# Experts over dispatched token blocks in plain fp32, rows scattered and added back by indirect DMAs

## The reference

```python
logits = x @ gate_weight.T                      # 1024 tokens, 28 experts
scores = softmax(logits)
topk_w, topk_idx = top_k(scores, 6)
topk_w = topk_w / (topk_w.sum(-1) + 1e-20)
cw = zeros(1024, 28); cw[token, topk_idx] = topk_w
for e in 28 experts:                            # w_gate, w_up 256x176, w_down 176x256
    h = silu(x @ w_gate[e]) * (x @ w_up[e])
    y = y + cw[:, e] * (h @ w_down[e])
```

## Time and profile before

| | us |
|---|---|
| median of 3 runs | 1101.35 |
| lowest, highest | 1100.94, 1104.36 |
| profiled execution | 1102.48 |
| its span | 1100.7 |
| PE busy in the span | 923.4 (84%) |
| DVE, ACT, POOL busy | 583.1, 399.9, 501.0 |
| 16 DMA engines, mean moved | 70 GB/s |

### The profile page before, as it was taken

The page is one execution under the profiler, slowest core; times in us unless marked ns, Lnnn a source line. Parts: engine busy times, 40 slices in busy tenths (PEclk is TensorE's granted clock), DMA queues, the critical chain, the costliest instruction groups (busy, mean ns, idle before and its releaser), DMA issues. The chain is left out here.

```text
span 1100.7 us, 14919 instructions
## 1 busy us (share of the span) xinstructions
PE 923.4 (84%) x5205; PEld 692.6 (63%) x5206; DVE 583.1 (53%) x1343; ACT 399.9 (36%) x1042; POOL 501.0 (46%) x492
## 2 busy tenths in 40 slices
PE   5898989885588876786898758998998988999998
PEld 3566766653457544554565436766766777888887
DVE  2367697965473885354475233554446464334333
ACT  2255554541022110231232113444444534444443
POOL 2256666752030233113124123455344556788875
PEclk9799989987689887779798758999999989999999
DMA  8030000022200200000000103333223324454442
GB/s 292 0 154 2 1 1 1 1 77 115 77 0 1 99 5 15 1 6 14 1 10 10 21 1 106 96 121 96 73 96 96 98 80 151 144 161 151 159 155 93
DMA packets 47103, 76.52 MB, mean 70 GB/s; under 512 B 21252, under 2 KB 24629, under 8 KB 46134
## 3 DMA queue, kind: packets, MB, share of 16 engines
q1 hardware_dynamic: 46308, 75.20, 21.4%
q10 hardware_dynamic: 722, 0.37, 0.1%
HBM read 73.35 MB, written 2.21 MB: 69 GB/s over the span
## 5 line engine op out<-in xcount | busy, mean ns | idle before, releaser
L791 PE MATMUL PS<-R 128*64 128x256 f32 (+7 forms) x992 | 141.1, 378 | 13.9 <-ACT R L1990 8.4
L1990 ACT ACTIVATE R<-PS 128x512 f32<-128x512 f32 (+5 forms) x183 | 87.8, 519 | 131.1 <-PE PS L791 72.6
L2418 POOL TENSOR_TENSOR R<-SelT,bqkv 128x1024 f32<-128x1024 f32 x32 | 64.2, 2027 | 155.3 <-DVE SelT L1810 93.2
L791 PE MATMUL PS<-xTh,uh 128*128 128x512 f32 x312 | 130.9, 420 | 2.1 <-POOL ul L2430 2.0
L791 PE MATMUL PS<-xTh,ul 128*128 128x512 f32 x312 | 124.8, 400 | 0.0
L791 PE MATMUL PS<-xTl,uh 128*128 128x512 f32 x312 | 124.7, 400 | 0.0
L2430 POOL TENSOR_TENSOR ul<-R,uh 128x512 fp32r<-128x512 f32 x78 | 100.6, 1290 | 37.8 <-ACT uh L1990 37.7
L791 PEld LDWEIGHTS PS<-R 128*64 128x64 f32 (+3 forms) x992 | 75.1, 158 | 65.5 <-issue 32.2
L799 PE MATMUL PS<-ident,R 128*128 128x128 f32 (+2 forms) x462 | 74.7, 299 | 49.5 <-ACT R L2232 22.4
L2351 POOL TENSOR_SCALAR R<-R 128x256 f32<-128x256 f32 x88 | 80.9, 937 | 61.8 <-DVE R L1508 61.8
L799 PEld LDWEIGHTS PS<-ident,R 128*128 128x128 f32 (+2 forms) x462 | 55.2, 151 | 73.9 <-ACT R L2232 31.3
(11 more groups left out here) (280 smaller groups left out, 1968.6 us busy)
## 6 DMA issues: line engine op xcount, KB each, us to landing
R<-in_wmo SPq DMA_DIRECT2D x78, 384.0 KB, 3.1
xh<-cwd SPq DMA_DIRECT2D x28, 256.0 KB, 3.3
R<-in_wqkv SPq DMA_DIRECT2D x1, 4096.0 KB, 13.2
xh<-cwd SPq DMA_DIRECT2D x14, 224.0 KB, 3.1
xh<-cwd SPq DMA_DIRECT2D x14, 192.0 KB, 3.1
xh<-cwd SPq DMA_DIRECT2D x14, 160.0 KB, 3.0
R<-in_wot SPq DMA_DIRECT2D x1, 2048.0 KB
bqkv<-in_bqkv SPq DMA_DIRECT2D x1, 2048.0 KB, 7.9
```

Source lines behind the costliest of these rows:

```text
L791: return e.matmul(out, l, r, start=start, stop=stop, skip_group_check=True)
L1990: return e.activation(out, a, ACT.Copy)
L2418: e.tensor_tensor(pv4(pr2, i % 2, "ghd"), Pg, vg, ALU.mult).then_inc(sem("m2"), 1)
```

## The change

The experts are computed only for the tokens that chose them. The chosen (token, expert) pairs are 1024 x 6 = 6144 rows. Each batch's router now finds the six indices (`max_index`), counts ranks with small matmuls (`rk`), works out each row's place in DRAM (`rt_p`) and scatters the rows of 258 words (256 features, the weight, the token's number) by 12 indirect DMAs on POOL (`sc`) into `xg`, where each expert has room for 1024 rows. SP fills `xg` and three accumulators `y0` to `y2` with blank rows at the start of the program (32 DMAs). `mp` works out, from the counts, which expert and which rows belong to each of 75 blocks of 128 rows; 75 = 48 full blocks + 27 is the most that there can be, and all 75 are run. A block's result is added to `y{j%3}` in DRAM by one indirect DMA with an add. At the end SP loads the three, DVE adds them to x.

`moe`, `l1x_late` and the split operands are gone. The cross attention of all four batches stands in one `l1x` beside `l1a` (ratio 0.8), and the experts follow it alone.

```diff
-NCH = 39
+NB = 75
+NW = 3
+NX = 8
+NY = 3
+    def experts():
+        add("mp", banks=[0, 1, 7])
+        for j in range(NX - 2):
+            add("ldx", j)
+        for j in range(NW):
+            add("ldw", j)
+        add("et", 0, banks=[0])
+        add("et", 1, banks=[1])
+        add("eu", 0, banks=[2])
+        for j in range(NB + 1):
+            if j + NX - 2 < NB:
+                add("ldx", j + NX - 2)
+            if j + 1 < NB:
+                add("eu", j + 1, banks=[2 + (j + 1) % 2])
+            if j < NB:
+                add("eh", j, banks=[4 + j % 2])
+            if j:
+                add("ed", j - 1, banks=[6 + (j - 1) % 2])
+                if j - 1 + NW < NB:
+                    add("ldw", j - 1 + NW)
+            if j + 2 < NB:
+                add("et", j + 2, banks=[j % 2])
+        add("out")
...
-    side = drive(l1x((0, 1), extra_), side, 0.75)
+    side = drive(l1x((0, 1, 2, 3), extra_), side, 0.8)
-    side = drive(moe(0), second(), RATIO)
-    drive(moe(1), None, 0)
+    experts()
...
 # SP
+            for ex in range(NE):
+                dst = D["xg"][ex * CAP:ex * CAP + CAP, :].rearrange("(c p) n -> p c n", p=128)
+                e.dma_start(dst, zrow[:, :].rearrange("p (o n) -> p o n", o=1).to_broadcast([128, 8, ROW])).then_inc(sem("init"), 16)
+            def ldx(j):
+                if j == 0:
+                    e.wait_ge(sem("blocks"), 1)
+                    e.wait_ge(sem("xg"), 16 * 48)
+                if j >= NX:
+                    i = j - NX
+                    e.wait_ge(sem(f"y{i % NY}"), 16 * (i // NY + 1))
+                r = e.value_load(blocks[0:1, 128 + j:129 + j], min_val=0, max_val=PAD)
+                e.dma_start(xb[j % NX], D["xg"][bass.ds(r, 128), :]).then_inc(sem(f"xb{j % NX}"), 16)
+            def ldw(j):
+                if j >= NW:
+                    u = fill("ed", j - NW)
+                    e.wait_ge(u.full, u.f + 1)
+                v = e.value_load(blocks[0:1, j:j + 1], min_val=0, max_val=NE - 1)
+                e.dma_start(wr_[j % NW], D["wgu"][bass.ds(v, 1)].rearrange("o p n -> (o p) n")).then_inc(sem(f"w{j % NW}"), 16)
+                e.dma_start(wr2[j % NW], D["wd2"][bass.ds(v, 1)].rearrange("o p n -> (o p) n")).then_inc(sem(f"w{j % NW}"), 16)
...
 # PE
+            def et(j):
+                u = fill("et", j)
+                e.wait_ge(sem(f"xb{j % NX}"), 16 * (j // NX + 1))
+                room(u)
+                for c in range(2):
+                    a = tr(u.t[:, c * 128:c * 128 + 128], xb[j % NX][:, c * 128:c * 128 + 128])
+                a.then_inc(u.full, 1)
+            def eu(j):
+                u, w = fill("eu", j), fill("et", j)
+                e.wait_ge(w.free, w.k + 1)
+                e.wait_ge(sem(f"w{j % NW}"), 32 * (j // NW + 1))
+                room(u)
+                for k in range(2):
+                    a = mm(u.t[:, 0:352], xbT[j % 2][:, k, :], wr_[j % NW][:, 352 * k:352 * k + 352], k == 0, k == 1)
+                a.then_inc(u.full, 1)
+            def eh(j):
+                u, w = fill("eh", j), fill("eu", j)
+                e.wait_ge(w.free, w.k + 1)
+                room(u)
+                tr(u.t[:, 0:128], hm[j % 2][:, 0:128])
+                tr(u.t[0:48, 128:256], hm[j % 2][:, 128:176]).then_inc(u.full, 1)
+            def ed(j):
+                u, w = fill("ed", j), fill("eh", j)
+                e.wait_ge(w.free, w.k + 1)
+                room(u)
+                mm(u.t[:, 0:256], hT_[j % 2][:, 0:128], wr_[j % NW][:, 704:960], True, False)
+                mm(u.t[:, 0:256], hT_[j % 2][0:48, 128:256], wr2[j % NW], False, True).then_inc(u.full, 1)
...
 # DVE: eu multiplies silu(gate) by up, eh copies hT_, ed scales by the token's weight
+            def ed(j):
+                u = fill("ed", j)
+                e.wait_ge(u.full, u.f + 1)
+                if j >= NY:
+                    e.wait_ge(sem(f"y{j % NY}"), 16 * (j // NY))
+                e.tensor_scalar(ys[j % NY], u.t[:, 0:256], xb[j % NX][:, 256:257], None, ALU.mult).then_inc(u.free, 1)
...
 # ACT: et copies xbT, eu takes silu of the gate half
...
 # POOL
+            def ed(j):
+                u = fill("ed", j)
+                e.wait_ge(u.free, u.k + 1)
+                if j >= NY:
+                    e.wait_ge(sem(f"y{j % NY}"), 16 * (j // NY))
+                e.indirect_dma_start(out=D[f"y{j % NY}"][:, :],
+                                     out_offset=bass.IndirectOffsetOnAxis(ap=xb[j % NX][:, 257:258].bitcast(I32), axis=0),
+                                     in_=ys[j % NY], in_offset=None, compute_op=ALU.add).then_inc(sem(f"y{j % NY}"), 16)
```

More of the change, by code:

```diff
@@ L58, in pair_banks @@
 def pair_banks(i):
[L60 to L71, removed]
+    return ((2, 3), (4, 5))[i % 2]
 def plan():
@@ L307, in ask @@
             for b in bs:
-                if b not in asked and b in x3:
+                if b not in asked and b in x3 and b <= now + 1:
                     asked.append(b)
@@ L339, in l1x @@
                 yield
[L341 to L358, removed]
     def done(b, p, extra_):
@@ L408, in plan @@
     extra_ = []
-    side = drive(l1x((0, 1), extra_), side, 0.75)
-    for _ in side or ():
-        pass
-    while 1 not in cwc:
+    side = drive(l1x((0, 1, 2, 3), extra_), side, 0.8)
+    assert side is None
+    while extra_:
         if next(extra_[0], "end") == "end":
             extra_.pop(0)
[L415 to L421, removed]
-    side = drive(moe(0), second(), RATIO)
-    for _ in side or ():
-        pass
-    drive(moe(1), None, 0)
+    experts()
     return p
@@ new lines, in mp @@
+            def mp():
+                u0, u1, u7 = fills("mp")
+                e.wait_ge(sem("SM"), 4)
+                room(u0)
+                mm(u0.t[0:28, 0:1], SM, ones[:, 0:1], True, True).then_inc(u0.full, 1)
+                e.wait_ge(sem("blk_n"), 1)
+                room(u1)
+                mm(u1.t[0:28, 0:1], utri2[0:28, 0:28], mpn[:, 1:2], True, True).then_inc(u1.full, 1)
+                e.wait_ge(u1.free, u1.k + 1)
+                room(u7)
+                mm(u7.t[0:1, 0:75], ones[0:28, 0:1], mpb, True, True)
+                mm(u7.t[0:1, 128:203], mpn[:, 2:3], mpb, True, True).then_inc(u7.full, 1)
@@ L1892, in rt_k @@
                 u = fill("rt_g", b)
+                e.wait_ge(u.free, u.k + 1)
                 got = [None, None]
-                def step(s, ins):
-                    own.mark(ins)
+                for s in range(2):
+                    own.mark(e.max(m8b[:, s, :], p30[s]))
                     got[s] = own.n
-                def after(s):
+                for s in range(2):
                     e.wait_ge(own.sem, got[s])
-                for s in range(2):
-                    if s == 0:
-                        e.wait_ge(u.free, u.k + 1)
-                    step(s, e.reciprocal(rr[s][:, 2:3], rr[s][:, 1:2]))
@@ L1918, in rt_k @@
-                for s in range(2):
-                    after(s)
-                    step(s, e.tensor_reduce(rr[s][:, 3:4], r30[s][:, 0:28], X, ALU.add))
-                for s in range(2):
-                    after(s)
-                    step(s, e.tensor_scalar(rr[s][:, 3:4], rr[s][:, 3:4], 1e-20, None, ALU.add))
-                for s in range(2):
-                    after(s)
-                    step(s, e.reciprocal(rr[s][:, 3:4], rr[s][:, 3:4]))
-                for s in range(2):
-                    if s == 0 and b:
-                        w = fill("rt_c", b - 1)
-                        e.wait_ge(w.full, w.f + 1)
-                    after(s)
-                    e.tensor_scalar(cwr[s], r30[s][:, 0:28], rr[s][:, 3:4], None, ALU.mult).then_inc(sem("cwr"), 1)
@@ L1963, in out @@
-            def out(hf):
-                us = fills("y0", hf)
-                e.wait_ge(sem("dn"), NCH * (hf + 1))
-                for q in range(2):
-                    t0 = 4 * hf + 2 * q
-                    xv_ = x[:, t0:t0 + 2, :]
-                    e.tensor_tensor(xv_, us[q].t[:, :].rearrange("p (q n) -> p q n", q=2), xv_, ALU.add).then_inc(us[q].free, 1)
+                    own.mark(e.max_index(ix8[:, s, :], m8b[:, s, :], p30[s]))
+                own.mark(e.tensor_reduce(rq[:, 0:2], m8b[:, :, 2:8], X, ALU.add))
@@ new lines, in ed, with out @@
+            def ed(j):
+                u = fill("ed", j)
+                e.wait_ge(u.full, u.f + 1)
+                if j >= NY:
+                    e.wait_ge(sem(f"y{j % NY}"), 16 * (j // NY))
+                e.tensor_scalar(ys[j % NY], u.t[:, 0:256], xb[j % NX][:, 256:257], None, ALU.mult).then_inc(u.free, 1)
+            def out():
+                for i in range(NY):
+                    e.wait_ge(sem(f"yb{i}"), 16)
+                    for q in range(4):
+                        xv_ = x[:, 2 * q:2 * q + 2, :]
+                        a = e.tensor_tensor(xv_, yb[i][:, 2 * q:2 * q + 2, :], xv_, ALU.add)
+                        if i < NY - 1:
+                            own.mark(a)
+                        else:
```

(13 more changed lines are left out.)

439 lines of the change are left out of this document (198 added, 241 removed).

## The result

| | us |
|---|---|
| before, median (lowest to highest) | 1102.86 (1100.94 to 1106.71) |
| after, median (lowest to highest) | 1510.12 (1506.61 to 1517.83) |
| after / before, 95% interval | 1.370 (1.363 to 1.376) |
| profiled execution of after, its span | 1510.95, 1508.9 |

The changed kernel is 37% slower. The forecast of 1400 us was 110 us too low; the time lies within its range. Matmuls now have line L757, transposes L765.

The account below looks back on a forecast made before the run. The prediction took PE to bound the dense experts before, and exposed weight loads to pace blocks after: blocks start at 760, plus 622 for 75 blocks and 15.5 tail, 1397, plus 1.8, called 1400 us; range from a little under 1220 to 1535.

Parts of the forecast that it names:

- 75 blocks: The expert block stage: 75 periods of 8.3 us, 622 us in all.
- The ring: Weights' ring of three places: nothing is fetched ahead, so each block pays the full way from `ed`'s end to landing.
- The landing way: In each block, from `ed`'s end to landed weights: semaphore 0.1, register 0.8, loads 3.5, together 4.4 us.
- The block's work: PE's `eu`, `eh` and `ed` in each block: 2.3 us at 2.4 GHz, divided by clock 0.6, 3.8 us.
- Rival 1: Block stage: PE's clock stays at 1.2 GHz throughout, 9.1 us a block, 1461 us in all; chance 20%.
- The start of the blocks: Everything ahead of the expert blocks, from cross attention through routers, scatters and first loads: blocks start at 760 us.
- 16 x 5.6: Cross attention of batches 2 and 3: 16 pairs at 5.6 us, 90 us; longer pairs would mean being wrong.
- The 5 us for all side effects: Ahead of the last scatter: POOL's scatters of batches 0 to 2 before norms, and 33 MB of blank rows; 0 to 20.
- Scatter and first loads: Before the first block: batch 3's 12 scatters with landing 15 us, then SP's first x and weight loads 12 us.
- Rival 2: Block stage: adding DMAs bind through SP's queue, deciding from a y way of 7.2 us; 1580 at 12; chance 15%.
- rival 3: Block stage: landings at their shortest and full clock, 5.9 us a block, 1220 us in all; chance 10%.
- Rival 4: Block stage: the ring hides the loads and PE sets about 3.4 us a block, 1033 us; chance 4%.

Follow-up runs that it names:

- ring6: Changed kernel with six places instead of three in the ring of weights: 1095.94 us, 0.991 of the kernel before.
- fixed_expert: Changed kernel with block j always taking expert j mod 28, so no register read for the weights: 1454.77 us, 1.317 of the kernel before.
- warm16: Changed kernel with sixteen unused bf16 matmuls on PE in the gap ahead of each `eu`: 1359.28 us, 1.231 of the kernel before.
- ring6_spread: ring6 with the 12 scatters of a batch issued one by one between cross attention steps: 1072.95 us, 0.971 of the kernel before.
- no_add: Changed kernel with block results written to y by the indirect DMAs without the add: 1529.13 us, 1.385 of the kernel before.
- ring4: Changed kernel with four places instead of three in the ring of weights: 1228.83 us, 1.112 of the kernel before.
- all_together: ring6 with spread scatters, `et` ahead of `eh`, and first weights asked ahead of the first x rows: 1056.01 us, 0.955 of the kernel before.
- all_x_later: all_together with x rows asked for four blocks ahead, not six: 1031.35 us, 0.936 of the kernel before.

## Why the prediction was right, and where it was off

It was right in kind: slower, because each block exposes its whole load. Its sum (1400) was 111 us short of the profiled 1510.95, and the wide range covered that. By its own parts:

| part | forecast | measured | difference |
|---|---|---|---|
| first `eu` | 760 | 805.4 | +45.4 |
| 75 blocks | 622 | 685.5 | +63.5 |
| tail to the end of the span | 15.5 | 18.0 | +2.5 |

**The ring.** Right. `ldw(n)` waits for `ed(n-3)`, and between that and `eu(n)` stands one `et`. ring6 takes that away alone, and 414 us go.

**The landing way, 4.4 us and 0.1 for the start.** Right: 4.47 in the middle of the blocks. Its terms hold as well: the register 0.67 to 0.71 (0.8 forecast, by fixed_expert), the two loads 3.5 (3.5).

**The block's work, 3.8 us.** This step failed: the work took 4.75 us in the mean, and these 0.95 us are nearly all of the period's excess. Both numbers of 2.3 / 0.6 were off. The sum of matmuls at the higher clock was short: warm16 shows 2.64 for the same burst. Most of that is `ed`, sized 0.85, which takes 1.16 there (1005.64 to 1006.80 in one block), since its last matmul has to be through. 2.64 / 0.6 = 4.4, an estimate by which this is 0.6 of the 0.95 us. The rest is the clock. The stage's mean was forecast well (0.6; 0.61 measured), but a mean over a stage holds the gaps as well, and a grant that falls into a gap gives nothing back. Windows of after: `eu` with `eh`, `ed`, the wait, and the next `eu`; then the same three of the second block after:

```profile
1207.10:1210.00 2.90, 2.90 (x7) 1.75 (x7) 0.00 (x0) 0.18 (x1) 0.00 (x0) 0.50 0.13 25
1210.00:1211.60 1.60, 1.60 (x7) 0.83 (x6) 0.83 (x4) 0.13 (x1) 0.00 (x0) 0.85 0.17 56
1212.40:1216.00 3.60, 0.00 (x0) 0.00 (x0) 0.00 (x0) 0.00 (x0) 1.41 (x1) 0.71 0.74 180
1216.10:1219.00 2.90, 2.90 (x7) 1.75 (x7) 0.00 (x0) 0.18 (x1) 0.00 (x0) 0.50 0.16 33
...
1225.40:1228.30 2.90, 2.90 (x7) 1.75 (x8) 0.00 (x0) 0.20 (x1) 0.00 (x0) 0.50 0.17 32
1228.30:1230.40 2.10, 2.10 (x5) 0.82 (x4) 0.73 (x3) 0.12 (x1) 0.00 (x0) 0.50 0.13 41
1230.50:1234.70 4.20, 0.61 (x2) 0.21 (x2) 0.48 (x1) 0.38 (x1) 1.55 (x1) 0.50 0.55 147
```

In the first of these blocks `eu` runs at 1.2 GHz (0.50), the higher clock is granted late in the burst (0.85), lasts into the wait (0.71), and is gone when the next `eu` starts. In the last block shown it isn't granted at all. So it goes throughout: of the 70 blocks from 829.95 us on, all have 0.50 or 0.51 over the first 2.9 us, and 30 have 0.50 to the end of the wait. The mean clock is 0.54 in the bursts and 0.68 in the gaps. By form the mean matmul of `eu` takes 826 / 478 = 1.73 times as long as in warm16, those of `ed` 609 / 428 = 1.42 and 578 / 380 = 1.52. So the work of a block came near the 4.6 that the prediction had for 1.2 GHz throughout (bursts that stay at 0.50 take 5.04). Rival 1 (9.1 us a block, given 20%) was nearer than the forecast (8.3). The Trainium skill's section "HAM oscillation — how this bites in real kernels" ("TensorE: Matmul & The Clock Gate") has PE restart throttled after each wait for DMA, and the trace agrees (0.50 or 0.51 in the first 2.9 us of each of these 70 bursts).

75 times the excess of the period, 9.29 - 8.3, would be 74 us. 63.5 came of it, since the first three loads are asked for together and only the later blocks wait for `ed`. The `eu` of blocks 0, 1 and 2 in after:

```profile
805.37 2.69 PE L757 MATMUL PS<-R,bqkv 128*128 128x352 f32 x4 [6.68 <-issue]
...
808.70 2.69 PE L757 MATMUL PS<-R,bqkv 128*128 128x352 f32 x4 [0.65 <-issue]
...
812.71 2.33 PE L757 MATMUL PS<-R,bqkv 128*128 128x352 f32 x4 [0.47 <-ACT bqkv L1997]
```

The first two periods take 7.3 us together, 11.2 less than two of 9.29. Nothing is saved at the end: from the last `eu` (1480.93) to the end of the last `ed` 10.0 us pass.

**The start of the blocks, 760.** The pairs were sized well: 5.7 and 5.2 us each within batches 2 and 3 (5.6 forecast). Wrong was 16 x 5.6: from the last pair of one batch to the first of the next, PE's `xs` steps are 39.3 us apart (590.39 to 629.69, batch 1 to 2) and 36.4 (669.91 to 706.36, batch 2 to 3), and the sum had 5.6 for each. So the 16 pairs took 152 us (590.39 to 742.49), 9.5 each, and more than 5.6 each was what the prediction had named as a sign of being wrong. Of the two distances, 16.4 and 18.1 us are the waits behind POOL's scatters; in ring6_spread the same distances are 26.8 and 20.4. The rest, 13 to 17 us each above a pair's 5.6, is `x_end`, norm and router of one batch and `x_pre` of the next, which the prediction costed for the last batch alone. Batch 1 being through 15 us sooner (its last pair starts at 590.39, not at 605.69 as in the earlier trace rows) gave some of it back. The 5 us for all side effects named the right queue and priced it at a seventh of its cost: it did not work out who waits behind twelve scatters in a row. The 33 MB of blank rows, in the same charge, cost nothing that shows: wqkv lands at 144 us, DMA is quiet from slice 5 on (151 us), and POOL's first product of the self attention starts at 392.7 us, 1.5 sooner than before.

**Scatter and first loads.** Right in sum: from the last `xs` to the first `eu` 64 us were forecast, 62.9 measured. A scatter's issue takes 0.96 us and 0.30 to the next, 1.27 in all (1.0 forecast).

**The rivals.** Rival 2 did not bind here (no_add), but its order did in ring4 and all_together; the y DMA's way from `ed`'s end was some 0.8 us to its issue (1211.4 to 1212.26 in the block shown) and 4.5 to its landing, 5.3 in all, below the 7.2 at which it was to decide. Neither condition of rival 3 came: the landing way was 4.47 us, not 3.5, and with full clock alone warm16 had 7.28 a block, not 5.9. Rival 4 named what a deeper ring shows: its 3.4 us a block stands beside ring6's 3.58.

## What to carry to other kernels

A ring's place that holds the operands of an early and of a late step is in use from the one to the other; count the steps between the release and the next use, and if there are next to none, each use pays the whole way of the load, however idle DMA is. Ask of every wait in a DMA-issuing queue, and of every long run of issues on a compute engine, what stands behind it: here these two cost 79 us (ring4) and 23 us (ring6). When bursts alternate with gaps, price the bursts at the clock that rows show inside a burst, not at the stage's mean.

## What the runs showed of the hardware

- The granted clock lags the work: with bursts of 4.75 us and gaps of 4.5 in the mean, it was 0.50 or 0.51 over the first 2.9 us of all 70 bursts, 0.54 over the bursts and 0.68 over the gaps. Useless matmuls in the gap gave 1.00 and 151 us back.
- An indirect DMA of 128 rows of about 1 KB occupies POOL for 0.96 us (plain) or 1.55 us (with an add), and the next follows 0.30 us later. The adding one landed after 4.5 us in after and 3.9 in fixed_expert, the writing one after 4.0 in no_add, so no price of the add shows in the landing.
- The 16 DMA engines reached a share of 1.00 at 258 GB/s with this mix of rows (all_x_later).
- A read of a register from SBUF on SP ahead of a DMA costs 0.67 to 0.71 us (after against fixed_expert).
